# A recurrent step on VectorE: one wait instead of two before four operations

## The reference, cut to what matters

```
def step(h, xs):
    xzt, xrt, xht = xs
    z = jax.nn.sigmoid(xzt + h @ U_z + vz)
    r = jax.nn.sigmoid(xrt + h @ U_r + vr)
    hh = jnp.tanh(xht + r * h @ U + vh)
    h_new = (1.0 - z) * h + z * hh
    return (h_new, h_new)
```

## Time and profile before

| | us |
|---|---|
| median of 3 runs | 2133.18 |
| lowest and highest | 2130.86, 2134.11 |
| the profiled execution | 2136.35 |
| its span in the trace | 2134.3 |
| the recurrence within the span, about | 21 to 1060 |

### The profile page before, as it was taken

One profiled execution on the slowest core, in us unless ns is written; L12 is line 12 of the kernel. 1 busy time (PEld: TensorE's weight loads), 2 busy tenths in 40 slices (PEclk: granted clock), 3 DMA queues, 4 the chain that ended last, 5 costly groups with the idle time before them and its releaser, 6 DMA issues. The chain is left out here.

```text
span 2134.3 us, 82919 instructions
## 1 busy us (share of the span) xinstructions
PE 2093.6 (98%) x32724; PEld 1970.2 (92%) x32732; DVE 1574.5 (74%) x8995; ACT 1025.5 (48%) x3981; POOL 415.6 (19%) x560
## 2 busy tenths in 40 slices
PE   8999999999999999999989999999999999999997
PEld 7899999999999999999768888767999999999997
DVE  6887877787777887788745555593777777777775
ACT  3565665665555655555555776532222222222221
POOL 0000000000000000000000000445455555555553
PEclk7555555555555555555599999999999999999999
DMA  3001000000000000000002322223888888888882
GB/s 127 4 4 44 4 4 4 4 4 4 4 4 4 4 4 4 4 4 4 3 1 90 112 85 80 107 70 132 299 268 276 279 267 277 279 267 278 277 264 58
DMA packets 55559, 213.72 MB, mean 100 GB/s; under 512 B 11579, under 2 KB 40961, under 8 KB 46977
## 3 DMA queue, kind: packets, MB, share of 16 engines
q1 hardware_dynamic: 36276, 184.41, 23.6%
q0 software_dynamic: 17408, 23.61, 5.9%
q10 hardware_dynamic: 1484, 0.40, 0.1%
HBM read 192.82 MB, written 15.57 MB: 98 GB/s over the span
## 5 line engine op out<-in xcount | busy, mean ns | idle before, releaser
L1895 PE MATMUL bank<-xe,ring 128*128 128x160 f32 x3072 | 438.7, 299 | 0.7 <-DVE xe L1953 0.7
L1895 PEld LDWEIGHTS bank<-xe,ring 128*128 128x128 f32 x3072 | 422.7, 190 | 0.9 <-issue 0.9
L1946 DVE STREAM_TRANSPOSE turned<-ye 32x64 f32<-32x64 f32 x1240 | 291.3, 235 | 16.2
L869 PEld LDWEIGHTS bank<-keep_part,Us 128*128 128x128 f16 x6120 | 276.0, 111 | 1.6 <-DVE keep_part L781 0.4
L1659 POOL MEMSET cum<- 128x320 f32 x1 | 0.4, 365 | 1350.4 <-POOLq L1051 1350.4
L869 PE MATMUL bank<-keep_part,Us 128*128 128x4 f16 x6120 | 259.3, 170 | 0.4 <-DVE keep_part L781 0.3
L1931 ACT ACTIVATE gate_f<-bank 128x160 f32<-128x160 f32 x384 | 116.4, 303 | 284.6 <-PE bank L1895 283.7
L869 PE MATMUL bank<-raw,Us 128*128 128x4 f16 x6132 | 242.6, 167 | 0.5 <-DVE raw L805 0.4
L1836 POOL DMA_INDIRECT out_rows<-res,to_row x128 | 192.3, 1502 | 229.6 <-issue 215.2
L510 ACT ACTIVATE r_h<-bank 128x8 f32<-128x8 f32 x512 | 92.8, 181 | 279.0 <-PE bank L869 278.5
L1906 PE MATMUL bank<-mid,ring 128*128 128x160 f32 x1536 | 219.1, 299 | 0.0
(11 more groups left out here) (279 smaller groups left out, 4047.6 us busy)
## 6 DMA issues: line engine op xcount, KB each, us to landing
ring<-in_ew SPq DMA_DIRECT2D x64, 2304.0 KB, 9.2
raw<-in_L_cond_ew SPq DMA_DIRECT2D x16, 1024.0 KB, 6.3
ctx_rows<-rows SPq DMA_DIRECT2D x2, 1280.0 KB, 7.0
dense_w<-in_L_ffn_W SPq DMA_DIRECT2D x2, 1024.0 KB, 9.4
dense_w<-in_L_cond_sw SPq DMA_DIRECT2D x2, 1024.0 KB, 6.4
out_rows<-res,to_row POOLq DMA_INDIRECT x128, 4.9
xT<-in_xT SPq DMA_DIRECT2D x2, 864.0 KB, 10.5
dense_w<-in_sw1T SPq DMA_DIRECT2D x1, 1536.0 KB, 11.1
```

Source lines behind the costliest of these rows:

```text
L869: last = nc.tensor.matmul(pre[g][q][:, jj, m, :], Us[:, g, p, k, m * P:(m + 1) * P], x[part][:, k * B:(k + 1) * B], start=False, stop=Fals ...
L1895: last = nc.tensor.matmul(bank[f % UPS][:, s_ * CAP:(s_ + 1) * CAP], w1[u][:, k, s_ * FFN + f * P:s_ * FFN + (f + 1) * P], xe[e % 2][:, k] ...
L1946: last = nc.vector.transpose(y[:, :, q, :], ye[e % 2][q * SQ:(q + 1) * SQ, :, j * SQ:(j + 1) * SQ])
```

## The change

Four waits are taken out. Each stood beside another wait of the same operation, on a semaphore that the same engine raises later:

- ahead of the scan for `rh_low`: `s_hr` (the copy of the state beside r, written in the step before by VectorE, ahead of L768, whose `s_rhhi` stays);
- ahead of L781: `s_khi` (L775), where `s_k` (L777) stays;
- ahead of L785: `s_z` (L515), where `s_c` (L517) stays, both of ScalarE;
- ahead of L805: `s_hhi` (L794), where `s_h` (L799) stays.

```
                     dve.wait_ge(s_rhhi, m)
-                    dve.wait_ge(s_hr, m)
                     low_part(rh_low, r_h, rh_high).then_inc(s_rhlo, 1)
...
-                    dve.wait_ge(s_khi, m)
                     dve.wait_ge(s_k, m)
                     nc.vector.tensor_tensor(keep_part[:, 1], keep[:], keep_part[:, 0], ALU.subtract).then_inc(s_klo, 1)

                     dve.wait_ge(s_c, m)
-                    dve.wait_ge(s_z, m)
                     nc.vector.tensor_tensor(step_high[:, :, 2], z, cand, ALU.mult).then_inc(s_shi, 1)
...
                     dve.wait_ge(s_h, m + 1)
-                    dve.wait_ge(s_hhi, m + 1)
                     nc.vector.scalar_tensor_tensor(out=part_of(1, j), in0=h_new, scalar=2.0, in1=part_of(0, j),
                                                    op0=ALU.mult, op1=ALU.subtract).then_inc(s_hlo, 1)
```

## The result

| | before | after |
|---|---|---|
| median of 20 runs | 2134.26 us | 2128.95 us |
| lowest to highest | 2130.86 to 2136.37 | 2126.12 to 2131.08 |
| ratio, with 95% interval | | 0.9975 (0.9969 to 0.9981) |
| the profiled execution, its span | 2136.35, 2134.3 | 2130.45, 2128.4 |
| recurrence, first to last start of step_high's operation | 1033.88 | 1028.30 |

The changed kernel is 0.25% faster. Of the 5.9 us between the two spans, 5.6 lie in the recurrence. The page of the changed kernel (to compare with the earlier trace rows): 2048 instructions fewer, the same clock picture but for one digit, and 17 packets fewer on the second instruction queue.

What follows compares the result with a forecast made beforehand. A ring of hand-offs between VectorE, TensorE and ScalarE was taken to bound the recurrence. Four waits at 0 and refills at -1.3 us gave 2135.1 for the profiled execution, 2132 us against the runs' median; range 2128 to 2136.

Steps and rivals of the forecast that it cites:

- the outcome that had a chance of 0.08: Whole kernel faster by more than 0.2%: 0.06 for waits holding VectorE's sequencer, 0.02 for a floor on issuing each instruction.
- all 5.2 us of the refills gone: VectorE's instruction fetches: all the extra time seen in 24 long steps vanishes, giving the range's low end, 2128 us.
- The ring of hand-offs: Recurrence step: VectorE, TensorE and ScalarE wait in turn; L785 and L768 start as soon as ScalarE allows, steps 2.00 us.
- Scan, z_done, h_hi: Waits ahead of rh_low's scan, L785 and L805: each taken as 0; bounds 1.0 us for the scan, 0.1 us for h_hi.
- The wait ahead of L781: Low part of keep on VectorE: starts about 0.07 us sooner, 0.19 behind L777's start, but off the path, worth 0.
- the rival that gave the 104 ns to the operation: Ahead of L781: the gap belongs to the operation, so it stays 0.27 us behind L777; 2132 us as well, chance 0.1.
- Fewer instructions to fetch: VectorE's instruction queue: 51 refills instead of 67 at about 0.08 us each, 1.3 us less.
- slower, the refills fall on the path: VectorE's recurrence steps: all 51 refills falling badly would add 12 us, 2145; chance of over 0.2% slower 0.06.
- faster, the sequencer is late: VectorE: every instruction removed shortens the step; 22 us gained if L805's wait held 330 steps, 2111 us; chance 0.06.
- the issue floor: VectorE's sequencer: about 20 cycles, 21 ns, per instruction; four fewer per step estimated at 43 us, 2090 us; chance 0.02.
- would not move: L781 on VectorE: by the skill page its start stays put; by the measured gap it moves 0.07 us; same sum either way.

Runs made afterwards that it cites:

- four met waits: Changed kernel with four more wait instructions per step, where the four were taken out, each on a value met long before; 0.9983 of before (0.9974 to 0.9992).

## Why the prediction was right or wrong

The forecast was 2132 us and no measurable change; it came to 2128.95 by the runs, faster by 5.3 us than the 20 runs of the kernel before, past the 4.3 set as the bound. So what came is, if only just (0.25%, interval 0.19 to 0.31, bound 0.2), the outcome that had a chance of 0.08, and neither of the two reasons given for it holds. The time lies in the range, near its low end, which was worked out as "all 5.2 us of the refills gone"; that is about what happened, though the prediction gave no reason why they should all go. That the number lies inside is luck besides: the three runs it started from have a median 1.1 us below that of the 20 (2133.18 against 2134.26); from the latter the same low end would have been 2129.1, just above what was measured.

- **The ring of hand-offs: right.** 511 of the 512 starts of L782 lie 0.03 or 0.04 us behind the end of L517 (493 of 503 did before by the prediction's count), and the plain step is 2.00 us as before.
- **Scan, z_done, h_hi: worth 0, right.** L801 follows L796 at 0.20 us as L805 followed L799 (851.74 against 851.54 in the step shown), and the 18.8 us idle ahead of the scan became 17.2; the difference is about what its long intervals had in them, 1.8 us.
- **The wait ahead of L781: right.** 0.19 us as forecast, so the rival that gave the 104 ns to the operation falls; 17.5 us of idle where "about 19" was said, and the 36.4 us that went are in the idle time ahead of L782 (+36.5). Left in alone, it costs nothing that shows.
- **Fewer instructions to fetch: right in kind, wrong in size, and this is the step that failed.** 1.3 us was forecast; it is 5.3 by the medians, 5.6 in the two traces. The number of refills went as said (block ends 15.2 us apart to 19.8, where "20" was said; 134 packets to 117). The error was "about 0.08 us for each of some 67 refills", a mean price taken from a list that was anything but uniform: 21 of 68 block ends were longer by 0.15 to 0.36 us, and they were those with a wait instruction in the last place. The trace had it in view: each of these 21 was longer by 0.154 us or more, none of the other 47 by more than 0.148. A sort of the list by pair of operations would have shown it; the earlier trace rows have two of the pairs. The changed kernel has about 0.25 wait instructions per step instead of 4.25, so among its 52 block ends about one of that kind was to be expected (there is one), and some 17 of 68 before (there are 21). How much the change gains is thus in part a matter of where the blocks of the kernel before happen to end: with its ends moved by 10 instructions it took 0.9995, by 5 it took 1.0014, and against those the changed kernel's 0.9975 would be 0.2% and about 0.4%.
- **The rival "slower, the refills fall on the path"** named the right mechanism: where the blocks end decides. With 5 instructions ahead of the loop the kernel before got 0.14% slower by it. It had it wrong that a refill in front of L785 costs nothing (0.15 to 0.17 us at five ends, one of them in the earlier trace rows), and it counted every operation as a place where one can fall badly; taking the waits out left a single bad end.
- **The rival "faster, the sequencer is late"** gave the right sign for a wrong reason; the median step stayed at 2.00 us, and of the 43 us that the issue floor would have given nothing is there.
- **The two places where the Trainium skill was weighed.** "VectorE: DVE Perf Modes", section "The DRAIN you can't avoid": that a chain takes as long with a semaphore after each operation as with one at the end isn't what this trace shows. Neighbours without a wait overlap (L776 starts 0.08 us behind L774 and L779, which carries its wait, 0.19 behind L776), and with a wait instruction on the value just raised it is 0.26. The forecast by the gap, 0.19 us, came out, the page's "would not move" did not. "Runtime: NRT & Kernel Launch", section "Instruction fetch mechanics": on this queue the blocks are of 128 instructions, not 256, since the long intervals stand at one place modulo 128 in all kernels, at odd and even multiples alike. That they are mostly hidden holds behind operations (0 of 51 long in the changed kernel), not behind a wait instruction (21 of 21).

## What to carry to other kernels

Off the path the direct gain is nothing, however large the gap ahead of the operation looked. Rare long intervals deserve a list by pair and by place in the queue before a mean price is put on them: here 21 of them were most of the effect, and five idle instructions ahead of the loop moved the whole kernel by 0.14%.

## What the hardware showed that I had not expected

The end of a block of 128 instructions on VectorE's queue is hidden behind operations (0 long of 51 in the changed kernel) and shows when a wait instruction is among the last of the block, met or not: up to 0.37 us in the last place, 0.30 in the last but one, 0.14 to 0.22 at ten of 52 ends with three operations in between, nothing that shows in the first place of the new block or 23 places away. Behind it stands one figure: 0.42 us from the record of the wait instruction in the last place to the next operation, in 137 of 139 block ends of 13 kernels. A wait instruction on the value that the operation just before raises delays the next operation by 67 ns against a wait that this operation carries; one on a value met long before, by nothing that shows away from a block's end (18.1 us of idle ahead of L781 with four met waits, 17.5 with none). Why the reading ahead doesn't go past a wait instruction stays open, as does whether the other engines' queues do the same.
